# A conv, attention and gated-FFN kernel: t1 centred by its weights, its mean carried in a 129th column, and three steps moved in the written order

## The chip, the cores and the metric

The kernel runs on one core of a Trainium2 chip. Five engines work side by side: TensorE (PE: matmuls; PEld: its weight loads), VectorE (DVE), ScalarE (ACT), GpSimd (POOL) and SyncE (SP, which issues all DMAs here). The metric is the device time of one execution in microseconds (us), lower is better.

## The reference, cut to what matters

```python
x = conv(x)                    # (I - circulant)^-1 over the 128 channels: a 128x128 matrix
t = to_tokens(x)               # 16 batches of 1024 tokens, 128 channels each
t = t + attention(_ln_t(t))    # causal linear attention, 8 heads, then W_out       -> "t1"
t = t + ffn(_ln_t(t))          # per batch: mean gate, merged W1 and W2, LN, gain, bias
x = from_tokens(t)

def _ln_t(v, eps=1e-05):
    m = mean(v, axis=-1); s = var(v, axis=-1)      # over the 128 channels of a token
    return (v - m) / sqrt(s + eps)
```

t1 is used twice: its normalised form z = (t1 - mean) * rstd feeds the gate and the FFN, and t1 itself is added to the FFN's result at the end.

## The kernel before

**Setup** (lines 199 to 364) computes the conv matrix from its filter, folds it into the weights that x meets (`wbig`, split into float16 high and low parts `wh` and `wl`: 128 columns of conv, then 384 of q, k and v), turns W_out into `woT`, and prepares constants. VectorE writes these one after another; a barrier ends it.

**Phase 1** (lines 367 to 1038) goes over 16 batches of 8 tiles of 128 tokens, 128 tiles in all. Each engine runs a written list of stages once per slot; a stage's number is its skew, the slots by which it lags tile t. So a slot is one tile's time, and in slot s a stage of skew k works on tile s - k. The engines meet by semaphores only. The stages that matter here:

- ACT: `v_hi`, `normalise` (z from t1, line 796: an Identity with a scale and a bias that are read per partition), `split_x` (every second slot, even), `tv_hi` (a piece of the FFN's weight share to float16, also even slots), `relu_qk`, `gate_relu` (odd slots), `read_t1` (t1 from PSUM, line 744), `exp_qk`, `state_hi`, two `scores_hi`, `copy_out`.
- DVE: `stats2`, `mean_var2` and `eps2` of t1, `shift2` (line 883: minus mean times rstd, one value a partition), `tv_lo` (line 846), two `scores_lo`, `make_qk`, `v_lo` and others.
- POOL: `split_x` (even slots), `rsqrt2`, `qk_hi` (line 1001), `z_hi` (line 1019), `qk_lo`, `z_lo`, `rsqrt1`.
- PE: `gate` (odd slots), `project`, `state`, `scores`, `turn_out`, `conv`, `values`, `out_project`. `conv` shares a PSUM bank with `out_project`, so it waits until `read_t1` of the slot has read the bank.
- SP: `turn` (q and k to the transposed layout by DMA), `turn_z`, `store` of t1 to DRAM, `load_x`, `load_tv`.

**Phase 2** (lines 1041 to 1438) goes over 32 half batches of 512 tokens, called q, again in slots. PE makes the hidden layer (`up_0` to `up_3`), then `down_0` to `down_3`; each `down` takes the high and low parts of the hidden layer, and the low parts (`h_lo`, line 1369) come from DVE. DVE's order in a slot is

```python
FFN_VECTOR_ORDER = [("copy_b1", 0), ("stats", 2), ("hidden_lo_0", 1), ("hidden_lo_2", 1), ("add_up", 3),
                    ("mean_var", 2), ("add_eps", 2), ("hidden_hi_1", 0), ("copy_w2", 0), ("shift", 2),
                    ("hidden_hi_3", 0), ("hidden_lo_1", 0), ("hidden_lo_3", 0)]
FFN_GPSIMD_ORDER = [("rsqrt", 2), ("gain", 2)]
```

`rsqrt` (line 1433) follows `add_eps`, `shift` (line 1397) follows `rsqrt`, ACT's `normalise` follows `shift`, `gain` (line 1426, POOL, times the LN gain) follows `normalise`, and `add_up` (line 1404, DVE) adds t1, which SP has loaded back from DRAM into `t1b` two half batches ahead.

Of the kernel before, what the change touches and what calls it, by code (L numbers as in the profile page):

```python
# [7 lines left out]
F32 = mybir.dt.float32  # L8
F16 = mybir.dt.float16
# [26 lines left out]
TVW = FO * C // B  # L36
PKW = 2 * (NH * 4 * DH + DH)
# [25 lines left out]
FFN_GPSIMD_ORDER = [("rsqrt", 2), ("gain", 2)]  # L63
# [52 lines left out]
def build(nc, d):  # L116

    top = ExitStack()
    with top:
# [14 lines left out]
        wh = sb(top, "w_in_hi", [P, 4 * C], F16)  # L134
        wl = sb(top, "w_in_lo", [P, 4 * C], F16)
        woT = sb(top, "w_outT", [P, C])
# [62 lines left out]
        with ExitStack() as su:  # L199
# [6 lines left out]
            yt = sb(early, "t1", [P, TILES, C])  # L206
# [9 lines left out]
            wbig = sb(su, "w_in", [P, 4 * C])  # L216
# [4 lines left out]
            with nc.Block() as block:  # L221
# [31 lines left out]
                def _(dve):  # L253
# [51 lines left out]
                    nc.vector.tensor_scalar(wbig[:, C:3 * C], pa[:, 4, 0:2 * C], WSI, None, ALU.mult)  # L305
                    link(nc.vector.tensor_scalar(wbig[:, 3 * C:4 * C], pa[:, 4, 2 * C:3 * C], WSI * VS, None, ALU.mult))
# [60 lines left out]
        with early, ExitStack() as pa_:  # L367
# [28 lines left out]
             t1_ready, bn2, mv2, ve2, rstd2, shift_ready, z_ready, zhi_ready, zlo_ready, gt_done, gate_ready) = [  # L396
# [4 lines left out]
                    "t1_ready bn2 mv2 ve2 rstd2 shift_ready z_ready zhi_ready zlo_ready gt_done gate_ready").split()]  # L401
# [38 lines left out]
            with nc.Block() as block:  # L440
                @block.sync
                def _(sp):
# [77 lines left out]
                def _(pe):  # L520
# [194 lines left out]
                def _(act):  # L715
# [111 lines left out]
                def _(dve):  # L827
# [104 lines left out]
                    def merged_w1(slot):  # L932
# [33 lines left out]
                        "make_qk": make_qk, "shift2": shift2, "state_lo": state_lo,  # L966
# [74 lines left out]
        with ExitStack() as pb:  # L1041
# [11 lines left out]
            t1b = sb(pb, "t1_back", [P, 2, HALF, C])  # L1053
# [62 lines left out]
            with nc.Block() as block:  # L1116
# [181 lines left out]
                def _(dve):  # L1298
# [121 lines left out]
                def _(pool):  # L1420
# [8 lines left out]

                    def rsqrt(g, pair, h):  # L1430
# [7 lines left out]
                    run(pool, FFN_GPSIMD_ORDER, {"rsqrt": rsqrt, "gain": gain})  # L1438
# [30 lines left out]
```

## Time and profile before

| | |
|---|---|
| three runs | 732.48, 734.12, 737.25 us; median 734.12 |
| the profiled execution | 735.35 us, its span 733.4 us |
| granted TensorE clock, mean | 0.983 |
| busy share: PE, DVE, ACT, POOL | 93%, 88%, 86%, 68% |

Lines are those of the kernel before. An instruction's span reaches past the start of the next one on its engine, since instructions overlap at their ends; so the time that one takes from its engine is read from start to start, and sums of spans overstate how full an engine is.

### The profile page before, as it was taken

The numbers are of one execution on the slowest core, as the hardware profiler recorded it, in microseconds if no ns is written. First come the engines' busy times: TensorE is split into PE (matmuls) and PEld (weight loads), VectorE is DVE, ScalarE is ACT, GpSimd is POOL, SyncE is SP. The second block draws the span as 40 slices with busy tenths as digits, with TensorE's granted clock in tenths as the row PEclk, the third lists the DMA queues.
The fourth block names the chain that finished last, engine by engine and source line by source line (L and its number), as shares of the span: only waits on it lengthen the run. The fifth ranks groups of instructions, "written<-read, shape, count | busy, mean of one in ns | idle before, by whom it ended". The sixth has DMA issues, their size and how long they took to land. (4 is left out here: it accounts for less than half of the span.)

```text
span 733.4 us, 39983 instructions
## 1 busy us (share of the span) xinstructions
PE 683.1 (93%) x13026; PEld 531.0 (72%) x13026; DVE 647.6 (88%) x2535; ACT 634.2 (86%) x1780; POOL 498.8 (68%) x911
## 2 busy tenths in 40 slices
PE   3898999999999999999999998889999998999993
PEld 2576777777777777777777776767777797777772
DVE  5689999999999999999999999667998977998983
ACT  3689999999999999999999998457888876888883
POOL 3669999999999999999999997301333312333333
PEclk9999999999999999999999999799999999999998
DMA  4547876666666666666666665210222211222222
GB/s 138 109 111 130 154 139 151 143 147 147 148 138 156 143 144 149 147 152 144 143 149 151 136 142 119 38 37 17 77 83 72 86 44 45 87 72 72 86 86 72
DMA packets 200294, 82.58 MB, mean 113 GB/s; under 512 B 174028, under 2 KB 187503, under 8 KB 200184
## 3 DMA queue, kind: packets, MB, share of 16 engines
q1 hardware_dynamic: 200248, 81.98, 47.7%
q8 instruction: 28, 0.46, 0.3%
q14 instruction: 18, 0.15, 0.1%
HBM read 22.69 MB, written 17.30 MB: 55 GB/s over the span
## 5 line engine op out<-in xcount | busy, mean ns | idle before, releaser
L900 DVE SCALAR_TENSOR_TENSOR scores_lo<-p_a,scores_hi 128x512 f16<-128x512 f32 x256 | 170.6, 677 | 1.2 <-ACT scores_hi L781 1.2
L781 ACT ACTIVATE scores_hi<-p_a 128x512 f16<-128x512 f32 x256 | 162.7, 646 | 4.9 <-PE p_a L617 4.8
L1433 POOL TENSOR_TENSOR ffn_rstd_shift<-ffn_rstd_shift,consts 128x4 f32<-128x4 f32 x32 | 36.8, 1150 | 110.9 <-DVE ffn_rstd_shift L1391 110.9
L1260 ACT ACTIVATE h_f<-psb,merged_b_of_batch 128x512 f32<-128x512 f32 x128 | 87.3, 712 | 11.7 <-PE psb L1196 10.1
L1215 PE MATMUL psb<-merged_W_of_batch,h_hi 128*128 128x128 f16 x512 | 94.5, 220 | 2.3 <-DVE h_lo L1369 1.6
L1369 DVE TENSOR_TENSOR h_lo<-h_f,h_hi 128x512 f16<-128x512 f32 x128 | 95.5, 785 | 1.3 <-ACT h_hi L1271 1.2
L1216 PE MATMUL psb<-merged_W_of_batch,h_hi 128*128 128x128 f16 x512 | 94.2, 220 | 0.0
L1217 PE MATMUL psb<-merged_W_of_batch,h_lo 128*128 128x128 f16 x512 | 94.2, 220 | 0.0
L634 PE MATMUL p_o<-v_parts,scores_hi 128*128 128x17 f16 x1024 | 90.4, 171 | 2.4 <-issue 0.6
L1001 POOL CAST qk_parts<-qk_f 128x512 f16<-128x512 f32 x128 | 78.3, 612 | 17.9 <-issue 15.7
L634 PEld LDWEIGHTS p_o<-v_parts,scores_hi 128*128 128x128 f16 x1024 | 81.6, 96 | 11.8 <-issue 9.2
L638 PE MATMUL p_o<-v_parts,scores_lo 128*128 128x17 f16 x1024 | 89.9, 170 | 0.0
L636 PE MATMUL p_o<-v_parts,scores_hi 128*128 128x16 f16 x1024 | 89.7, 170 | 0.0
L1007 POOL TENSOR_TENSOR qk_parts<-qk_f,qk_parts 128x256 f16<-128x256 f32 x128 | 86.0, 672 | 0.6
L636 PEld LDWEIGHTS p_o<-v_parts,scores_hi 128*128 128x128 f16 x1024 | 80.4, 96 | 0.7 <-issue 0.7
L980 POOL TENSOR_TENSOR stats<-stats,consts 128x1 f32<-128x1 f32 x128 | 70.4, 550 | 15.4 <-DVE stats L853 15.0
L1426 POOL TENSOR_TENSOR normed<-normed,ln_gain_rows 128x512 f32<-128x512 f32 x32 | 40.6, 1269 | 59.0 <-ACT normed L1280 59.0
L638 PEld LDWEIGHTS p_o<-v_parts,scores_lo 128*128 128x128 f16 x1024 | 80.1, 96 | 0.0
L1280 ACT ACTIVATE normed<-psb,ffn_rstd_shift 128x128 f32<-128x128 f32 x128 | 48.2, 457 | 34.0 <-DVE ffn_rstd_shift L1397 34.0
L986 POOL TENSOR_TENSOR stats<-stats,consts 128x1 f32<-128x1 f32 x128 | 70.4, 550 | 4.3 <-DVE stats L859 4.3
L796 ACT ACTIVATE z<-t,stats 128x128 f32<-128x128 f32 x128 | 71.6, 560 | 0.0
L760 ACT ACTIVATE exp_qk<-p_in,stats 128x256 f32<-128x256 f32 x128 | 66.5, 520 | 5.8 <-POOL stats L980 5.0
(214 smaller groups left out, 2775.3 us busy)
## 6 DMA issues: line engine op xcount, KB each, us to landing
x_f<-in_x SPq DMA_DIRECT2D x32, 256.0 KB, 3.0
t_rows<-t SPq DMA_DIRECT2D x64, 128.0 KB, 2.0
t_back<-t_rows SPq DMA_DIRECT2D x32, 256.0 KB, 2.6
out<-out_tile SPq DMA_DIRECT2D x32, 256.0 KB, 2.0
tv_share<-in_L_ffn_tv_W SPq DMA_DIRECT2D x32, 128.0 KB, 2.2
qkT_parts<-qk_parts SPq DMA_TRANSPOSE x128, 3.1
zT_hi_lo<-z_parts SPq DMA_TRANSPOSE x64, 2.4
merged_W<-in_L_ffn_W SPq DMA_DIRECT2D x2, 256.0 KB, 4.3
```

The lines of the kernel that those rows point to most:

```text
L634: mm(num[:, h, :], hi, vp[:, t, h, 0:VW], start=(h == 0), stop=False, skip_group_check=True)
L636: mm(num[:, h, 0:DH], hi, vp[:, t, h, VW:VW + DH], start=False, stop=False, skip_group_check=True)
L638: last = mm(num[:, h, :], lo, vp[:, t, h, 0:VW], start=False, stop=True, skip_group_check=True)
L781: nc.scalar.activation(ah[:, t % 2, cols], p_a[:, cols], ACT.Relu).then_inc(ahi_ready[eo], 1)
L900: nc.vector.scalar_tensor_tensor(al[:, t % 2, cols], p_a[:, cols], 0.0, ah[:, t % 2, cols], ALU.max, ALU.subtract).then_inc(alo_ready[eo], 1)
L1001: nc.gpsimd.tensor_copy(parts_of(t % 4, 0, NH * 4 * DH + DH, 2 * DH), src.unsqueeze(2).broadcast_to([P, 2 * NH, 2, DH])).then_inc(qkhi_rea ...
L1007: nc.gpsimd.tensor_tensor(parts_of(t % 4, 2 * DH, NH * 4 * DH - 2 * DH, DH), qk[:, t % 4, :].rearrange("p (w h i) -> p w h i", w=2, i=DH), ...
L1215: mm(o, hi, w2b[:, bb, 0, c, :], start=False, stop=False)
L1216: mm(o, hi, w2b[:, bb, 1, c, :], start=False, stop=False)
L1217: last = mm(o, lo, w2b[:, bb, 0, c, :], start=False, stop=(c == FC - 1))
L1260: nc.scalar.activation(hf_[:, c, :], ps[:, c, :], ACT.Relu, bias=b1s[:, h // 2, c:c + 1], scale=1.0 / WS).then_inc(h_ready[c], 1)
L1369: nc.vector.tensor_tensor(hl[:, h % 2, c, :], hf_[:, c, :], hh[:, h % 2, c, :], ALU.subtract)\
```

## The change

The conv weights lose their mean over the output channels, W_out likewise, so that t1 comes out of PE without its channel mean. The mean itself is made as a 129th column (`C1` = 129) of the same four matmuls. `read_t1` copies 129 columns, the store to DRAM and the load back carry 1032 bytes for two tiles' rows where they carried 1024, `normalise` needs no bias, and `shift2` is gone. In phase 2 a new POOL step `add_mean` adds the 129th column to t1's 128 in place, before `add_up`. The lists of ACT, DVE and SP are written anew: `tv_hi` lags by one slot (odd slots, with `gate_relu`), `tv_lo` by two, `mean_var2` stands before `v_lo`, `turn` lags by three and stands first on SP.

```diff
-SCALAR_ORDER = [("v_hi", 2), ("normalise", 10), ("split_x", 0), ("tv_hi", 0), ("relu_qk", 2), ("gate_relu", 14),
+SCALAR_ORDER = [("v_hi", 2), ("normalise", 10), ("tv_hi", 1), ("split_x", 0), ("relu_qk", 2), ("gate_relu", 14),
                 ("read_t1", 7), ("exp_qk", 1), ("state_hi", 3), ("scores_hi_0", 4), ("copy_out", 6),
                 ("scores_hi_1", 4)]
-VECTOR_ORDER = [("invert", 6), ("stats2", 8), ("divide", 6), ("make_qk", 2), ("v_lo", 2), ("mean_var2", 8),
-                ("state_lo", 3), ("stats1", 0), ("tv_lo", 0), ("eps2", 8), ("shift2", 9), ("mean_var1", 0),
-                ("scores_lo_0", 4), ("eps1", 0), ("scores_lo_1", 4)]
+VECTOR_ORDER = [("invert", 6), ("stats2", 8), ("divide", 6), ("make_qk", 2), ("mean_var2", 8), ("v_lo", 2),
+                ("state_lo", 3), ("stats1", 0), ("tv_lo", 2), ("eps2", 8), ("mean_var1", 0), ("scores_lo_0", 4),
+                ("eps1", 0), ("scores_lo_1", 4)]
-SYNC_ORDER = [("turn_z", 12), ("store", 7), ("turn", 2), ("load_x", 3), ("load_tv", 1)]
+SYNC_ORDER = [("turn", 3), ("store", 7), ("turn_z", 12), ("load_x", 2), ("load_tv", 1)]
...
-FFN_GPSIMD_ORDER = [("rsqrt", 2), ("gain", 2)]
+FFN_GPSIMD_ORDER = [("add_mean", 2), ("rsqrt", 2), ("gain", 2)]
...
-                    nc.vector.tensor_scalar(wbig[:, 0:C], pa[:, 1, 0:128], WSI, None, ALU.mult)
+                    nc.vector.tensor_scalar(wbig[:, 0:C], pa[:, 1, 128:256], WSI, None, ALU.mult)
+                    link(nc.vector.tensor_reduce(wom[:, 2:3], pa[:, 1, 0:128], AX.X, ALU.add))
+                    nc.vector.tensor_scalar(wbig[:, C:Q0], wom[:, 2:3].broadcast_to([P, Q0 - C]), WSI / C, None, ALU.mult)
                     link(nc.vector.tensor_copy(gfh[:, :], wsqT[:, 4, :]))
                     dve.wait_ge(s_wtc, 1)
-                    nc.vector.tensor_scalar(woT[:, :], wsqT[:, 3, :], WSI, None, ALU.mult)
+                    link(nc.vector.tensor_reduce(wom[:, 0:1], wsqT[:, 3, :], AX.X, ALU.add))
+                    link(nc.vector.tensor_scalar(wom[:, 1:2], wom[:, 0:1], 1.0 / C, None, ALU.mult))
+                    nc.vector.tensor_scalar(woT[:, 0:C], wsqT[:, 3, :], wom[:, 1:2], WSI, ALU.subtract, ALU.mult)
+                    nc.vector.tensor_scalar(woT[:, C:C1], wom[:, 1:2], WSI, None, ALU.mult)
...
-                        o, cols = p_m1[:, 0:P], slice(j * P, (j + 1) * P)
-                        mm(o, xh[:, hf, cols], wh[:, 0:C], start=True, stop=False)
+                        o, cols = p_m1[:, 0:C1], slice(j * P, (j + 1) * P)
+                        mm(o, xh[:, hf, cols], wh[:, 0:C1], start=True, stop=False)
...
-                        nc.scalar.activation(yt[:, t, :], p_m1[:, 0:P], ACT.Copy, scale=1.0 / WSI).then_inc(t1_ready, 1)
+                        nc.scalar.activation(yt[:, t, :], p_m1[:, 0:C1], ACT.Copy, scale=1.0 / WSI).then_inc(t1_ready, 1)
...
-                        act.wait_ge(shift_ready, n + 1)
+                        act.wait_ge(rstd2, n + 1)
                         at_least(act, zlo_ready, n - 1)
-                        nc.scalar.activation(z_[:, t % 2, :], yt[:, t, :], ACT.Identity, bias=st2[:, t % 4, 10:11],
-                                             scale=st2[:, t % 4, 8:9]).then_inc(z_ready, 1)
+                        nc.scalar.activation(z_[:, t % 2, :], yt[:, t, 0:C], ACT.Copy, scale=st2[:, t % 4, 8:9])\
+                            .then_inc(z_ready, 1)
...
-                    def shift2(b, t):
-                        n = TILES * b + t
-                        dve.wait_ge(rstd2, n + 1)
-                        nc.vector.tensor_scalar(st2[:, t % 4, 10:11], st2[:, t % 4, 6:7], -1.0, st2[:, t % 4, 8:9],
-                                                ALU.mult, ALU.mult).then_inc(shift_ready, 1)
...
                         dve.wait_ge(gain_ready, q + 1)
-                        dve.wait_ge(t1_loaded[hf], 16 * (2 * pair + h // 2 + 1))
-                        nc.vector.tensor_tensor(rn[:, hf, :, :], rn[:, hf, :, :], t1b[:, hf, :, :], ALU.add)\
+                        dve.wait_ge(raised, q + 1)
+                        nc.vector.tensor_tensor(rn[:, hf, :, :], rn[:, hf, :, :], t1b[:, hf, :, 0:C], ALU.add)\
                             .then_inc(v_ready, 1)
...
+                    def add_mean(g, pair, h):
+                        q, hf = HB * pair + h, h % 2
+                        pool.wait_ge(t1_loaded[hf], 16 * (2 * pair + h // 2 + 1))
+                        nc.gpsimd.tensor_tensor(t1b[:, hf, :, 0:C], t1b[:, hf, :, 0:C],
+                                                t1b[:, hf, :, C:C1].broadcast_to([P, HALF, C]), ALU.add)\
+                            .then_inc(raised, 1)
...
-                    run(pool, FFN_GPSIMD_ORDER, {"rsqrt": rsqrt, "gain": gain})
+                    run(pool, FFN_GPSIMD_ORDER, {"rsqrt": rsqrt, "gain": gain, "add_mean": add_mean})
```

## Rows read from the trace of the kernel before

**Rows 1.** Windows: PE, PEld, DVE, ACT, POOL busy (instructions); clock; DMA share; GB/s.

```profile
200.00:250.00 50.00, 48.80 (x1162) 38.17 (x1162) 48.70 (x215) 49.76 (x163) 48.34 (x99) 1.00 0.65 149
...
540.00:600.00 60.00, 59.78 (x742) 47.25 (x740) 51.61 (x159) 50.13 (x99) 20.74 (x17) 1.00 0.23 75
```

**Rows 2.** Timeline of ACT, phase 1 (start, length, instruction).

```profile
305.82 0.51 ACT L796 ACTIVATE z<-t,stats 128x128 f32<-128x128 f32 x1
306.20 0.43 ACT L725 ACTIVATE x_hi<-x_f 128x256 f16<-128x256 f32 x1
306.51 0.32 ACT L734 ACTIVATE tv_hi<-tv_share 128x128 f32 x1
306.71 0.46 ACT L767 ACTIVATE p_in<-p_in,stats 128x256 f32<-128x256 f32 x1
...
328.93 0.46 ACT L751 ACTIVATE v_parts<-p_in,stats 128x128 f16<-128x128 f32 x1
355.79 0.46 ACT L751 ACTIVATE v_parts<-p_in,stats 128x128 f16<-128x128 f32 x1
```

**Rows 3.** Waits, 200 to 400 us: total, times, longest.

```profile
POOL qk_parts L1001 <- issue: 7.0, 30, 0.3
...
PEld p_m L557 <- ACT t L744: 3.1, 15, 0.2
```

**Rows 4.** Timeline of POOL, phase 2, one slot (in brackets: idle before, releaser).

```profile
579.65 1.27 POOL L1426 TENSOR_TENSOR normed<-normed,ln_gain_rows 128x512 f32<-128x512 f32 x1 [1.81 <-ACT normed L1280]
583.24 1.14 POOL L1433 TENSOR_TENSOR ffn_rstd_shift<-ffn_rstd_shift,consts 128x4 f32<-128x4 f32 x1 [2.33 <-DVE ffn_rstd_shift L1391]
586.20 1.27 POOL L1426 TENSOR_TENSOR normed<-normed,ln_gain_rows 128x512 f32<-128x512 f32 x1 [1.82 <-ACT normed L1280]
```

**Rows 5.** Timeline of DVE, phase 2, the same slot.

```profile
578.29 1.29 DVE L1369 TENSOR_TENSOR h_lo<-h_f,h_hi 128x512 f16<-128x512 f32 x2
...
580.37 1.71 DVE L1369 TENSOR_TENSOR h_lo<-h_f,h_hi 128x512 f16<-128x512 f32 x2
581.99 0.68 DVE L1404 TENSOR_TENSOR normed<-normed,t_back 128x512 f32<-128x512 f32 x1
582.59 0.37 DVE L1385 BATCH_NORM_AGGREGATE ffn_mean_var<-ffn_stats 128x2 f32<-128x6 f32 x4
583.00 0.17 DVE L1391 TENSOR_SCALAR ffn_rstd_shift<-ffn_mean_var 128x4 f32<-128x4 f32 x1
...
583.57 0.28 DVE L1353 COPY merged_W_of_batch<-merged_W_hi 128x512 f16 x1
```

**Rows 6.** Groups by line, 200 to 400 us: busy, mean ns, idle.

```profile
L796 ACT ACTIVATE z<-t,stats 128x128 f32<-128x128 f32 x60 | 34.3, 572 | 0.0
...
L751 ACT ACTIVATE v_parts<-p_in,stats 128x128 f16<-128x128 f32 x60 | 27.1, 452 | 0.0
...
L744 ACT ACTIVATE t<-p_m 128x128 f32<-128x128 f32 x60 | 19.3, 322 | 0.0
...
L883 DVE TENSOR_SCALAR stats<-stats 128x1 f32<-128x1 f32 x60 | 12.2, 204 | 0.0
```

**Rows 7.** DMA issues of the page (KB each, us to landing).

```profile
t_back<-t_rows SPq DMA_DIRECT2D x32, 256.0 KB, 2.6
...
qkT_parts<-qk_parts SPq DMA_TRANSPOSE x128, 3.1
```

**Rows 8.** Timeline of DVE, setup.

```profile
9.71 0.28 DVE L289 TENSOR_SCALAR cas_scaled<-consts,filter_steps 128x128 f32<-128x128 f32 x1
...
12.04 0.60 DVE L299 TENSOR_SCALAR w_outT<-square_weights_T 128x128 f32<-128x128 f32 x1
```

**Rows 9.** Timelines of POOL and DVE, phase 1: z_hi alone, and beside tv_lo.

```profile
318.31 0.30 POOL L1019 CAST z_parts<-z 128x128 f16<-128x128 f32 x1
...
321.63 0.36 DVE L846 SCALAR_TENSOR_TENSOR tv_lo<-tv_share,tv_hi 128x128 f32 x1
...
321.78 0.36 POOL L1019 CAST z_parts<-z 128x128 f16<-128x128 f32 x1
```

More of the change, by code:

```diff
@@ L36 @@
 TVW = FO * C // B
+C1 = C + 1
+Q0 = C + 16
 PKW = 2 * (NH * 4 * DH + DH)
@@ L133, in build @@
         delta2h = sb(top, "delta2_f16", [P, GB, FI], F16)
-        wh = sb(top, "w_in_hi", [P, 4 * C], F16)
-        wl = sb(top, "w_in_lo", [P, 4 * C], F16)
-        woT = sb(top, "w_outT", [P, C])
+        wh = sb(top, "w_in_hi", [P, Q0 + 3 * C], F16)
+        wl = sb(top, "w_in_lo", [P, Q0 + 3 * C], F16)
+        woT = sb(top, "w_outT", [P, C1])
         gfh = sb(top, "gate1_hi", [P, C], F16)
@@ L205, in build @@
             vp = sb(early, "v_parts", [P, 8, NH, 2 * DH + 1], F16)
-            yt = sb(early, "t1", [P, TILES, C])
+            yt = sb(early, "centred_t1_and_mean", [P, TILES, C1])
             g2n = sb(early, "gate2_rows", [E, C])
@@ L215, in build @@
             casd = sb(su, "cas_scaled", [P, 2, C])
-            wbig = sb(su, "w_in", [P, 4 * C])
+            wbig = sb(su, "w_in", [P, Q0 + 3 * C])
+            wom = sb(su, "w_out_mean", [P, 3])
             cw = sb(su, "centred_inverse", [P, C])
@@ L304, in _ @@
                     dve.wait_ge(s_pch, 3)
-                    nc.vector.tensor_scalar(wbig[:, C:3 * C], pa[:, 4, 0:2 * C], WSI, None, ALU.mult)
-                    link(nc.vector.tensor_scalar(wbig[:, 3 * C:4 * C], pa[:, 4, 2 * C:3 * C], WSI * VS, None, ALU.mult))
+                    nc.vector.tensor_scalar(wbig[:, Q0:Q0 + 2 * C], pa[:, 4, 0:2 * C], WSI, None, ALU.mult)
+                    link(nc.vector.tensor_scalar(wbig[:, Q0 + 2 * C:Q0 + 3 * C], pa[:, 4, 2 * C:3 * C], WSI * VS, None, ALU.mult))
                     link(nc.vector.tensor_copy(wh[:, :], wbig[:, :]))
@@ L395, in build @@
              av_done, den2, o_ready, ot_done, oT_ready, wo_done,
-             t1_ready, bn2, mv2, ve2, rstd2, shift_ready, z_ready, zhi_ready, zlo_ready, gt_done, gate_ready) = [
+             t1_ready, bn2, mv2, ve2, rstd2, z_ready, zhi_ready, zlo_ready, gt_done, gate_ready) = [
                 sem(s) for s in (
@@ L569, in project @@
                         cols = slice(j * P, (j + 1) * P)
-                        mm(p_in[:, t % 2, 0:3 * C], xh[:, hf, cols], wh[:, C:4 * C], start=True, stop=False)
-                        mm(p_in[:, t % 2, 0:3 * C], xh[:, hf, cols], wl[:, C:4 * C], start=False, stop=False)
-                        mm(p_in[:, t % 2, 0:3 * C], xl[:, hf, cols], wh[:, C:4 * C], start=False, stop=True).then_inc(in_done, 1)
+                        mm(p_in[:, t % 2, 0:3 * C], xh[:, hf, cols], wh[:, Q0:Q0 + 3 * C], start=True, stop=False)
+                        mm(p_in[:, t % 2, 0:3 * C], xh[:, hf, cols], wl[:, Q0:Q0 + 3 * C], start=False, stop=False)
+                        mm(p_in[:, t % 2, 0:3 * C], xl[:, hf, cols], wh[:, Q0:Q0 + 3 * C], start=False, stop=True).then_inc(in_done, 1)
                     def state(b, t):
@@ L657, in out_project @@
                         bank_read("out_project", n, t)
-                        o, cols = p_m1[:, 0:P], slice(j * P, (j + 1) * P)
-                        mm(o, xh[:, hf, cols], wh[:, 0:C], start=True, stop=False)
-                        mm(o, xh[:, hf, cols], wl[:, 0:C], start=False, stop=False)
-                        mm(o, xl[:, hf, cols], wh[:, 0:C], start=False, stop=False)
+                        o, cols = p_m1[:, 0:C1], slice(j * P, (j + 1) * P)
+                        mm(o, xh[:, hf, cols], wh[:, 0:C1], start=True, stop=False)
+                        mm(o, xh[:, hf, cols], wl[:, 0:C1], start=False, stop=False)
+                        mm(o, xl[:, hf, cols], wh[:, 0:C1], start=False, stop=False)
                         pe.wait_ge(oT_ready, n + 1)
@@ L920, in stats2 @@
                         dve.wait_ge(t1_ready, n + 1)
-                        nc.vector.bn_stats(st2[:, t % 4, 0:6], yt[:, t, :]).then_inc(bn2, 1)
+                        nc.vector.bn_stats(st2[:, t % 4, 0:6], yt[:, t, 0:C]).then_inc(bn2, 1)
                     def mean_var2(b, t):
@@ L965, in _ @@
                     run(dve, VECTOR_ORDER, {"tv_lo": tv_lo, "stats1": stats1, "mean_var1": mean_var1, "v_lo": v_lo,
-                        "make_qk": make_qk, "shift2": shift2, "state_lo": state_lo,
+                        "make_qk": make_qk, "state_lo": state_lo,
                         "scores_lo_0": scores_lo(0), "scores_lo_1": scores_lo(1),
@@ L1052, in build @@
             hl = sb(pb, "h_lo", [P, 2, FC, 512], F16)
-            t1b = sb(pb, "t1_back", [P, 2, HALF, C])
+            t1b = sb(pb, "t1_back", [P, 2, HALF, C1])
             rn = sb(pb, "normed", [P, 2, HALF, C])
@@ L1061, in build @@
             (b1_ready, gs_ready, g_done, g9r, b12_done, b_chain, gb_ready,
-             w2_copied, f2_done, fbn, fmv, fve, frs, fsh, n_ready, gain_ready, v_ready,
+             w2_copied, f2_done, fbn, fmv, fve, frs, fsh, n_ready, raised, gain_ready, v_ready,
              t_done, ob_ready) = [sem(s) for s in (
                 "b1_ready gs_ready g_done g9_ready b12_done b_chain gb_ready "
-                "w2_copied f2_done fbn fmv fve frs fsh n_ready gain_ready v_ready "
+                "w2_copied f2_done fbn fmv fve frs fsh n_ready raised gain_ready v_ready "
                 "t_done ob_ready").split()]
@@ L1462 @@
         aps[name[3:]] = nc.dram_tensor(name, a.shape, mybir.dt.from_np(a.dtype), kind="ExternalInput").ap()
-    aps["t1"] = nc.dram_tensor("t1_rows", (NHALF * P, HALF * C), F32, kind="Internal").ap()
+    aps["t1"] = nc.dram_tensor("t1_rows", (NHALF * P, HALF * C1), F32, kind="Internal").ap()
     aps["base_parts"] = nc.dram_tensor("base_parts", (2, 2, P, BW), F16, kind="Internal").ap()
```

4 lines of the change are left out of this document (2 added, 2 removed).

## Prediction

> **What bounds the kernel now.** I read the windows first, for a picture by stage. Phase 1 fills the time to about 445 us and shows four engines near full: of 50 us, ACT 49.76, PE 48.80, DVE 48.70, POOL 48.34; phase 2 shows PE 59.78 of 60 and POOL only 20.74 [rows 1]. Neither tells the bound, because spans overlap at their ends. So I read timelines from start to start next. In phase 1 a batch of 8 tiles takes 355.79 - 328.93 = 26.86 us, that is 6.7 us for a pair of slots (even and odd), and ACT's `normalise` takes 306.20 - 305.82 = 0.38 us of it per slot, `tv_hi` 0.20 us in the even slot [rows 2]. The list of waits then shows who is late: in even slots PE's `conv` waits for `read_t1` (15 times in 30 pairs), which on ACT stands behind `normalise`, `split_x`, `tv_hi` and `relu_qk`. So ACT's even slot sets the pair. POOL is nearly full as well: its only steady idle time is 7.0 us in 200, before `qk_hi`, once a pair [rows 3].
>
> Phase 2 is bound by a loop through DVE and POOL, though PE looks full. A slot is 586.20 - 579.65 = 6.55 us, from one `gain` to the next [rows 4]. DVE goes through it in order: two `h_lo` (1.29 us), stats, two more `h_lo`, `add_up`, `mean_var`, `add_eps` at 583.00 [rows 5]; then POOL's `rsqrt` at 583.24, `shift`, ACT's `normalise`, and `gain` [rows 4]. What to see is the second pair of `h_lo`: 1.71 us where the same two took 1.29 [rows 5]. It was issued at 580.37, while `gain` ran from 579.65 to 580.92. The first of the pair lost 0.42 us; it took its normal course only from about 580.79, 0.13 us ahead of `gain`'s end. So a VectorE instruction with two SBUF inputs stands still while such a GpSimd one runs. That lost time is already part of the loop, and the loop has no idle time on DVE except the wait for `rsqrt`.
>
> **Phase 1.** `normalise` loses its bias. The nearest rows for what is left: `v_parts` (one per-partition operand) 452 ns against `t` (none) 322 ns, so one operand costs 130 ns at most; z, with two, has 572 ns [rows 6]. I take 0.09 us off per tile, half of what z's 0.38 us a start has above `tv_hi`'s 0.20 us, which has no such operand and also reads SBUF [rows 2]; the bounds are 0 and 0.13. `tv_hi` leaves the even slot for the odd one: 0.20 us off the slot that PE waits for, 0.20 us on the other. So the even path to `read_t1` becomes 0.29 us shorter, which is more than the wait that it causes. `shift2` (204 ns long [rows 6], some 0.12 us a start) goes from DVE, and with it a step between `rsqrt2` and `normalise`. The 129th column adds one column of 128 to four matmuls and to `read_t1`: under 1% of 322 ns, nothing. Next late is POOL: it can give no more than its idle time, 7.0 us of 200 [rows 3], which over some 400 us of steady batches is 14 us. I take 12 us off. Bounds: 14 us off, and 7 us on, if the odd slot, now with `gate_relu` and `tv_hi`, becomes the long one (0.20 - 0.09 = 0.11 us for each of 60 pairs).
>
> The SP list looks rewritten, but the sequence hardly moves: between one `turn` and the next stand the same `store` or `turn_z`; only the two loads change places, each one turn earlier or later, and what they wait for (POOL's `split_x`, DVE's `tv_lo`) stands ahead of the `qk_lo` that the next `turn` waits for. `turn` lands 3.1 us after issue [rows 7], and its reader `scores` stands two slots behind `qk_lo`, so some tenths of a microsecond more would cost nothing. Moving `tv_lo` and `mean_var2` keeps each in its slot's slack. The longer rows of t1 (1032 bytes for 1024) go through stores that are read a whole batch later, and loads that land in 2.6 us [rows 7]; a load is issued when `add_up` ends (582.67 [rows 5]) and wanted when the next `gain` ends (587.47 [rows 4]), some 2 us after it has landed. All this I cost at nothing; its cover is POOL's pace.
>
> **Setup.** DVE's chain there is continuous to its end. Added: two reductions of 128x128 at 0.28 us [rows 8] plus links, three tiny scalings at about 0.1; `woT` gets cheaper, since at 0.60 us for a 0.28 us shape [rows 8] it had stood still beside POOL. Sum +0.8 us (0.3 to 1.5).
>
> **Phase 2, add_mean.** On POOL it is a 128x512 add like `gain`, 1.27 us, and stands right behind it, where POOL is idle for 2.33 us before `rsqrt` [rows 4]. By POOL's own row it costs nothing. But in that gap DVE runs `h_lo_0` (let go at 580.79), `h_lo_2` and `add_up`, all with two SBUF inputs, back to back until 582.6 [rows 5]. `add_mean` can't run beside them: one of the sides stands still. Which one, no row shows for this pair; the nearest is phase 1, where `tv_lo`, issued at 321.63 ahead of `z_hi` at 321.78, went first, and `z_hi` took 0.36 us for 0.30 [rows 9]. The earlier issued goes first. `add_mean` is issued at about 580.9, behind `h_lo_0` but ahead of `h_lo_2` (581.39). So I take it that `h_lo_2` stands still for it: gain's 1.27 less the 0.13 at its end, less up to 0.14 for a start already made, 1.0 to 1.14, say 1.07 us a slot. `h_lo_2` is in the loop, and `add_up`, `mean_var`, `rsqrt` and PE's `down_0` queue behind it. Of 32 half batches some 29 meet it: the first and the ends of the two groups don't. 29 x 1.07 = 31 us on. Bounds: nothing, and 29 x 1.27 = 37 us.
>
> The Trainium skill, SBUF — State Buffer, section "Who interferes with whom", speaks against the change: VectorE with two SBUF inputs and a GpSimd instruction that reads SBUF share a port under an exclusive lock, the second to issue blocks until the first has finished, and issue order decides. The trace agrees in the stall of 0.42 us [rows 5]. By the rule `add_mean` goes ahead of `h_lo_2`, as in the sum; it doesn't say whether a waiting GpSimd instruction gets in between two VectorE instructions that follow each other closely, on which the first rival rests.
>
> **The rivals.**
> - *VectorE keeps the port* through `h_lo_2` and `add_up`. Then `add_mean` runs from about 582.5 to 583.75, and `rsqrt`, behind it on POOL, starts 0.5 us late. 29 x 0.5 = 14.5 us on instead of 31: 737.5 us, no change. For it: two `h_lo` take 1.29 us together [rows 5], with no gap between them. Against: [rows 9], and POOL has waited since 580.9.
> - *The port is not held*, the rival on the other side: `add_mean` passes beside VectorE as `rsqrt` does, beside which a copy keeps its 0.28 us [rows 4, 5]. It then fits into the 2.33 us at no cost, and only phase 1 and the setup count: 723 us. It decides if `add_mean` takes under 0.4 us a slot from the loop (12 us over 29 slots). Against: `gain`, same shape and inputs, did hold `h_lo_0`.
> - *The gain of phase 1 is not there*: the odd slot becomes the long one, 0 to 7 us on, and phase 2 costs its 31 us: 766 to 773 us.
> - *The change doesn't do what it says*: `normalise` costs the same without its bias. Then only the 0.20 us of `tv_hi` helps; 3 to 4 us of the 12 are lost: 757 us, inside the forecast's own range.
>
> **How the numbers follow.** The profiled execution, 735.35 us (span 733.4 and 1.95 around it), stands 1.2 above the median of the runs. 735.35 + 0.8 - 12 + 31 = 755.2; less 1.2 is 754 us. Its own range is 748 to 761. With 14.5 for 31: 737.5; with 0: 723. Chances: forecast 0.46 (the fourth rival in it), VectorE keeps the port 0.25, port not held 0.21, no gain in phase 1 0.08. About 1% is what a measurement here tells from no change, 726.8 to 741.5. Slower: 0.46 + 0.08 + 0.02 of the first rival's upper end = 0.56; same 0.23; faster 0.21. The range from 722 to 763 leaves out half of the third case and most of the last.
>
> **What would show it.** Right: in phase 2 the gap from one `gain` to the next grows from 6.55 to 7.6 us, `h_lo` next to `add_mean` shows about 1.7 us, PE waits for `h_lo`; in phase 1 a batch takes 26.1 us, z some 480 ns, and POOL's idle time before `qk_hi` is gone. If VectorE keeps the port, `add_mean` shows a long span and `rsqrt` starts late by 0.5. A batch still at 26.8 us would mean that the odd slot took over. A load of t1 that lands later than `gain`'s end would put a wait before `add_mean`.

## The result, and the profile after

The changed kernel takes 752.05 us (median of 6 runs, 748.12 to 754.61) against 734.63 us of the kernel before (6 runs beside it): the ratio is 1.0229, 95% interval 1.0190 to 1.0268. It is slower by 2.3%, and the forecast was 754.

Where the time went is read from two steady stretches, since one execution's ends of phases scatter (POOL's first instruction of phase 2 starts at 471.35 to 473.96 us in six kernels with the same phase 1) while a slot in its steady part repeats to 0.02 us (one or two slots in four are 0.1 to 0.17 us longer, and such slots stand in the kernel before too). In phase 1 the batch of 8 tiles went from 26.82 us (mean of the later batches; 26.86 in the one of [rows 2]) to 26.43. In phase 2 the slot went from 6.55 us [rows 4] to 7.40. Over 15 and 29 of them that is 15 x 0.39 = 5.9 us off and 29 x 0.85 = 24.7 us on. The setup put some 0.7 us on (the first `v_parts` of phase 1 starts at 20.2 to 21.1 us in ten kernels with the new arithmetic, at 19.6 to 20.5 in four with the old). Sum: 19.5 on, where the interval says 14.0 to 19.7 and the spans of the two profiled executions differ by 18.8.

The slot of phase 2, first POOL's timeline (start, length, instruction, in brackets the idle time before and its releaser):

```profile
552.45 1.27 POOL L1428 TENSOR_TENSOR normed<-normed,ln_gain_rows 128x512 f32<-128x512 f32 x1 [1.82 <-ACT normed L1282]
553.67 1.49 POOL L1435 TENSOR_TENSOR t_back<-t_back 128x512 f32<-128x512 f32 x1
556.88 1.14 POOL L1442 TENSOR_TENSOR ffn_rstd_shift<-ffn_rstd_shift,consts 128x4 f32<-128x4 f32 x1 [1.72 <-DVE ffn_rstd_shift L1393]
559.84 1.27 POOL L1428 TENSOR_TENSOR normed<-normed,ln_gain_rows 128x512 f32<-128x512 f32 x1 [1.82 <-ACT normed L1282]
```

and DVE's in the same slot:

```profile
553.17 2.54 DVE L1371 TENSOR_TENSOR h_lo<-h_f,h_hi 128x512 f16<-128x512 f32 x2
555.63 0.68 DVE L1406 TENSOR_TENSOR normed<-normed,t_back 128x512 f32<-128x512 f32 x1
556.24 0.36 DVE L1387 BATCH_NORM_AGGREGATE ffn_mean_var<-ffn_stats 128x2 f32<-128x6 f32 x4
556.63 0.17 DVE L1393 TENSOR_SCALAR ffn_rstd_shift<-ffn_mean_var 128x4 f32<-128x4 f32 x1
...
558.06 0.16 DVE L1399 SCALAR_TENSOR_TENSOR ffn_rstd_shift<-ffn_mean_var,ffn_rstd_shift 128x4 f32<-128x4 f32 x1 [0.36 <-POOL ffn_rstd_shift L1442]
```

POOL's `add_mean` (line 1435) is hidden on POOL: there is still 1.72 us of idle time before `rsqrt`. What grew is the second pair of `h_lo`, 2.54 us where [rows 5] has 1.71. What follows it on DVE up to `shift` keeps its length and is late by as much. The chain that ended last (start, length, what) is now strung on that instruction, about once a slot:

```profile
546.79 1.52 DVE h_lo L1371
554.19 1.52 DVE h_lo L1371
```

The second `h_lo` of the pair takes 1.52 us here, 0.68 in the kernel before, and the starts lie 7.40 us apart: that is the new slot. Next comes the list of waits from 475 to 740 us (total, times, longest), first of the kernel before, then of the changed one, where PE's `down` matmuls wait for `h_lo` in nearly every slot:

```profile
PE psb L1215 <- DVE h_lo L1369: 1.6, 1, 1.6
```

```profile
PE psb L1217 <- DVE h_lo L1371: 25.7, 29, 1.5
```

And an `add_mean` with nothing beside it, the first of the phase, behind its load:

```profile
475.93 1.04 POOL L1435 TENSOR_TENSOR t_back<-t_back 128x512 f32<-128x512 f32 x1 [1.67 <-DMA t_back<-t_rows]
```

It takes 1.04 us alone, not `gain`'s 1.27 [rows 4]; so of the 1.49 that it has in a steady slot 0.45 are waiting, behind the first `h_lo` of the pair. In phase 1 the groups of 300 to 400 us (busy, mean ns, idle) show the cheaper `normalise`:

```profile
L804 ACT ACTIVATE z<-centred_t_and_mean,stats 128x128 f32<-128x128 f32 x30 | 13.3, 445 | 0.0
```

`normalise` takes 445 ns for 572 [rows 6], and from start to start 0.29 us for 0.385: 0.09 us off each, as forecast. The batch lost only 0.39 us, though, where 8 x 0.09 for `normalise` alone would be 0.72, and 0.29 for each of 4 even slots would be 1.16.

### The profile page after: what moved, and what is told of

Same layout as the page of the kernel before. It is cut to its first block and busy times, and to the rows that moved or that the text cites. A ratio compares the mean times of both kernels' runs of the same rounds, so it can differ in the third digit from the quotient of the medians.

```text
span 752.2 us, 39879 instructions
## 1 busy us (share of the span) xinstructions
PE 680.6 (90%) x13026; PEld 530.6 (71%) x13026; DVE 666.4 (89%) x2412; ACT 625.6 (83%) x1780; POOL 541.1 (72%) x943
## 5 line engine op out<-in xcount | busy, mean ns | idle before, releaser
L789 ACT ACTIVATE scores_hi<-p_a 128x512 f16<-128x512 f32 x256 | 157.6, 618 | 7.1 <-PE p_a L625 6.0
L1371 DVE TENSOR_TENSOR h_lo<-h_f,h_hi 128x512 f16<-128x512 f32 x128 | 120.4, 980 | 0.7 <-ACT h_hi L1273 0.6
L1217 PE MATMUL psb<-merged_W_of_batch,h_hi 128*128 128x128 f16 x512 | 95.4, 221 | 25.7 <-DVE h_lo L1371 25.7
L982 POOL TENSOR_TENSOR stats<-stats,consts 128x1 f32<-128x1 f32 x128 | 69.6, 543 | 18.9 <-DVE stats L861 16.7
L1217 PEld LDWEIGHTS psb<-merged_W_of_batch,h_hi 128*128 128x128 f16 x512 | 50.5, 99 | 31.4 <-DVE h_lo L1371 30.9
L988 POOL TENSOR_TENSOR stats<-stats,consts 128x1 f32<-128x1 f32 x128 | 68.9, 538 | 5.0 <-DVE stats L867 5.0
L768 ACT ACTIVATE exp_qk<-p_in,stats 128x256 f32<-128x256 f32 x128 | 63.0, 492 | 4.7 <-POOL stats L982 4.0
```

The costliest lines, as they stand in the source:

```text
L789: nc.scalar.activation(ah[:, t % 2, cols], p_a[:, cols], ACT.Relu).then_inc(ahi_ready[eo], 1)
L1217: mm(o, hi, w2b[:, bb, 0, c, :], start=False, stop=False)
L1371: nc.vector.tensor_tensor(hl[:, h % 2, c, :], hf_[:, c, :], hh[:, h % 2, c, :], ALU.subtract)\
```

## The experiments

### Phase 2: what add_mean costs, and why

**Without it.** The mean is not added back.

```diff
-FFN_GPSIMD_ORDER = [("add_mean", 2), ("rsqrt", 2), ("gain", 2)]
+FFN_GPSIMD_ORDER = [("rsqrt", 2), ("gain", 2)]
...
-                        dve.wait_ge(raised, q + 1)
+                        dve.wait_ge(t1_loaded[hf], 16 * (2 * pair + h // 2 + 1))
```

> The changed kernel without add_mean: the mean is not added back in phase 2, so that part of the computation is left out, and add_up waits for the load of t1 itself. Port theory (add_mean stands VectorE's second pair of h_lo still, 0.91 us a slot over 28 slots = 25.5 us): phase 2 falls back to about 253.5 us and the time to about 752.0 - 25.5 = 726.5 us; the second pair of h_lo goes back from 2.62 to 1.71 us. Rival, the longer rows of t1 (1032 bytes, a later landing, a strided operand) or the new order of the wait are what phase 2 pays for: then 740 to 752 us.

Measured: 728.37 us, ratio 0.9937 (0.9911 to 0.9963); slot 6.55 us, second pair of `h_lo` back at its old length:

```profile
557.05 1.70 DVE L1371 TENSOR_TENSOR h_lo<-h_f,h_hi 128x512 f16<-128x512 f32 x2
```

So `add_mean` is the whole of phase 2's cost. The longer rows of t1, their later landing and the moved wait cost nothing that shows. The ratio also gives what phase 1 brings, net of the setup: 4.6 us, 2.7 to 6.5 by its interval.

**As long, but without reading.** A one-column add takes the wait, and a memset has the length (0.95 us). The mean is not added back.

```diff
+            idle = sb(pb, "written_only", [P, 1025])
...
-                        nc.gpsimd.tensor_tensor(t1b[:, hf, :, 0:C], t1b[:, hf, :, 0:C],
-                                                t1b[:, hf, :, C:C1].broadcast_to([P, HALF, C]), ALU.add)\
-                            .then_inc(raised, 1)
+                        nc.gpsimd.tensor_tensor(idle[:, 1024:1025], t1b[:, hf, 0, 0:1], t1b[:, hf, 0, C:C1], ALU.add)
+                        nc.gpsimd.memset(idle[:, 0:1024], 0.0).then_inc(raised, 1)
```

> The changed kernel with add_mean replaced by a GpSimd memset of 128x1024 (about 1 us, it reads no SBUF) behind a one-column add that takes the wait; the mean is not added back, that part is left out. Port theory: POOL is busy for as long, but VectorE isn't stood still: h_lo back at 1.71 us, about 726 to 729 us. Rival, POOL's own time and order cost it (rsqrt late behind a 1 us operation, add_up late behind its signal): about 750 us, with h_lo short and rsqrt's wait longer.

Measured: 727.80 us, ratio 0.9931 (0.9905 to 0.9958), slot 6.55 us. POOL's and DVE's timelines:

```profile
561.72 0.64 POOL L1436 TENSOR_TENSOR written_only<-t_back 128x1 f32<-128x1 f32 x1
562.29 0.95 POOL L1437 MEMSET written_only<- 128x1024 f32 x1
```

```profile
561.20 1.70 DVE L1372 TENSOR_TENSOR h_lo<-h_f,h_hi 128x512 f16<-128x512 f32 x2
562.83 0.68 DVE L1407 TENSOR_TENSOR normed<-normed,t_back 128x512 f32<-128x512 f32 x1
```

POOL is busy as long, in the same place, with the same signal behind it, and nothing is slower. Beside the memset DVE's two-input instructions keep their 1.70 and 0.68 us. So it is neither POOL's time nor its order nor `add_up`'s wait, but what the add reads. The Trainium skill, SBUF — State Buffer, section "Who interferes with whom", has it so: a VectorE instruction with two SBUF inputs contends with a GpSimd instruction that reads SBUF, not with one that only writes. This pair of runs agrees, with 1.70 us for 2.54.

**Behind rsqrt instead of ahead of it.** The computation is whole.

```diff
-FFN_GPSIMD_ORDER = [("add_mean", 2), ("rsqrt", 2), ("gain", 2)]
+FFN_GPSIMD_ORDER = [("rsqrt", 2), ("add_mean", 2), ("gain", 2)]
```

> The changed kernel with GpSimd's list turned so that add_mean is issued behind rsqrt and ahead of gain, beside the later hi copies and the first pair of h_lo and not in the gap before rsqrt. Theory that the place in the list is the fault (add_mean in the rsqrt loop): about 727 us, because POOL is idle there for 1.7 us while ACT normalises. Port theory: the hold only moves from the second pair of h_lo to the work of VectorE that now lies beside it; shift and the first h_lo pair are in the same loop, so 740 to 752 us, and the second pair of h_lo is back at 1.71 us.

Measured: 752.64 us, ratio 1.0283 (1.0233 to 1.0332), slot 7.39 us. POOL's and DVE's timelines:

```profile
562.94 1.03 POOL L1435 TENSOR_TENSOR t_back<-t_back 128x512 f32<-128x512 f32 x1
```

```profile
558.86 1.78 DVE L1371 TENSOR_TENSOR h_lo<-h_f,h_hi 128x512 f16<-128x512 f32 x2
...
563.00 1.00 DVE L1399 SCALAR_TENSOR_TENSOR ffn_rstd_shift<-ffn_mean_var,ffn_rstd_shift 128x4 f32<-128x4 f32 x1 [0.91 <-POOL ffn_rstd_shift L1442]
563.92 0.41 DVE L1363 CAST h_hi<-h_f 128x512 f16<-128x512 f32 x1
```

The place in the list is not the fault: the same 0.84 us has moved. `shift`, an instruction of four columns that took 0.16 us, started 0.06 us behind `add_mean` and took 1.00, until `add_mean` had ended. The second pair of `h_lo`, here without `add_mean` beside it, is back at 1.78. `shift` is in the loop too, so the slot is the same to 0.01 us.

**The mean added on VectorE**, by four `scalar_tensor_tensor` in place of `add_up`'s one instruction; the computation is whole.

```diff
-FFN_GPSIMD_ORDER = [("add_mean", 2), ("rsqrt", 2), ("gain", 2)]
+FFN_GPSIMD_ORDER = [("rsqrt", 2), ("gain", 2)]
...
-                        dve.wait_ge(raised, q + 1)
-                        nc.vector.tensor_tensor(rn[:, hf, :, :], rn[:, hf, :, :], t1b[:, hf, :, 0:C], ALU.add)\
-                            .then_inc(v_ready, 1)
+                        dve.wait_ge(t1_loaded[hf], 16 * (2 * pair + h // 2 + 1))
+                        for j in range(HALF):
+                            last = nc.vector.scalar_tensor_tensor(rn[:, hf, j, :], t1b[:, hf, j, 0:C], t1b[:, hf, j, C:C1],
+                                                                  rn[:, hf, j, :], ALU.add, ALU.add)
+                        last.then_inc(v_ready, 1)
```

> The changed kernel with the mean added on VectorE instead: add_up becomes four scalar_tensor_tensor of 128x128 (t1 + mean column + normalised), GpSimd has no add_mean. Full computation. Port theory: no hold, but four instructions for one in the loop, some 0.2 to 0.3 us a slot more in add_up: 726.5 + 29 x 0.25 = about 733 us. Theory that the mean's work itself costs wherever it is put: about 750 us.

Measured: 740.52 us, ratio 1.0128 (1.0074 to 1.0183); 7 us above what was expected. The four take

```profile
558.53 1.13 DVE L1407 SCALAR_TENSOR_TENSOR normed<-t_back,normed 128x128 f32<-128x128 f32 x4
```

1.13 us where `add_up` took 0.68 [rows 5], and the slot is 7.00 us: all of the 0.45 us is in the loop (29 x 0.45 = 13 us). The mechanism held; the price had been put at half.

**The mean added on ScalarE**, where ACT waits for `shift`; the computation is whole.

```diff
-FFN_GPSIMD_ORDER = [("add_mean", 2), ("rsqrt", 2), ("gain", 2)]
+FFN_GPSIMD_ORDER = [("rsqrt", 2), ("gain", 2)]
...
+                    def add_mean(g, pair, h):
+                        q, hf = HB * pair + h, h % 2
+                        act.wait_ge(t1_loaded[hf], 16 * (2 * pair + h // 2 + 1))
+                        for j in range(HALF):
+                            last = nc.scalar.activation(t1b[:, hf, j, 0:C], t1b[:, hf, j, 0:C], ACT.Identity,
+                                                        bias=t1b[:, hf, j, C:C1], scale=1.0)
+                        last.then_inc(raised, 1)
...
-FFN_SCALAR_ORDER = [("hidden_3", 0), ("hidden_1", 0), ("hidden_hi_0", 0), ("hidden_0", 0), ("normalise", 2),
+FFN_SCALAR_ORDER = [("hidden_3", 0), ("hidden_1", 0), ("hidden_hi_0", 0), ("hidden_0", 0), ("add_mean", 2), ("normalise", 2),
```

> The changed kernel with the mean added on ScalarE: four activations of 128x128 (t1 plus its mean column as bias) ahead of normalise in ACT's list of phase 2, where ACT waits 1.06 us a slot for shift; GpSimd has no add_mean. Full computation. Port theory: ACT takes no part in the port that VectorE and GpSimd share, so the second pair of h_lo is back at 1.7 us; four activations take about 1.0 us from start to start (0.25 us each, as v_parts), which the wait hides: 727 to 730 us. Rival (ACT's wait isn't spare, since hidden_2 and hidden_hi_2 behind it come later): up to 1 us a slot, 740 to 755 us.

Measured: 730.26 us, ratio 0.9972 (0.9954 to 0.9990): the one full version that is faster than the kernel before by its interval, though by 0.3% only. ACT's timeline:

```profile
560.47 0.78 ACT L1262 ACTIVATE h_f<-psb,merged_b_of_batch 128x512 f32<-128x512 f32 x1
561.04 1.36 ACT L1281 ACTIVATE t_back<-t_back 128x128 f32<-128x128 f32 x4
562.40 1.51 ACT L1290 ACTIVATE normed<-psb,ffn_rstd_shift 128x128 f32<-128x128 f32 x4
```

The four take 1.36 us, not 1.0, and fill ACT's wait to its end: `normalise` follows with no gap. So the slot is 6.60 us, 0.05 over the one before (29 x 0.05 = 1.5 us).

### Phase 1: where the other half of the gain went

**tv_hi alone moved**, in the kernel before.

```diff
-SCALAR_ORDER = [("v_hi", 2), ("normalise", 10), ("split_x", 0), ("tv_hi", 0), ("relu_qk", 2), ("gate_relu", 14),
+SCALAR_ORDER = [("v_hi", 2), ("normalise", 10), ("tv_hi", 1), ("split_x", 0), ("relu_qk", 2), ("gate_relu", 14),
...
-                ("state_lo", 3), ("stats1", 0), ("tv_lo", 0), ...
+                ("state_lo", 3), ("stats1", 0), ("tv_lo", 2), ...
```

> The kernel before with tv_hi alone moved (one tile later, ahead of x_hi, so that it falls into the odd slot) and tv_lo two tiles later behind it; nothing else of the change. Theory of the prediction (ACT's even slot up to read_t1 sets the pair): 0.20 us for each of some 60 pairs, 12 us off, 723 to 727 us, the start of phase 2 at 468 to 472 us for 479.85. Rival (PE's conv of the even slot waits as much for x_lo, which stands on POOL behind rsqrt1 and z_lo and doesn't move with ACT): 0 to 3 us off, 731 to 735 us, phase 2 from 477 to 480 us.

Measured: 730.77 us, ratio 0.9984 (0.9965 to 1.0003); batch 26.77 us, 0.05 off. The even slots fell from 3.29 us to 3.08 and the odd ones rose from 3.46 to 3.66. To see why, the even slot before (ACT, POOL, PE):

```profile
319.51 0.45 ACT L725 ACTIVATE x_hi<-x_f 128x256 f16<-128x256 f32 x1
319.82 0.34 ACT L734 ACTIVATE tv_hi<-tv_share 128x128 f32 x1
...
320.37 0.32 ACT L744 ACTIVATE t<-p_m 128x128 f32<-128x128 f32 x1
...
320.09 0.68 POOL L1033 TENSOR_TENSOR x_lo<-x_f,x_hi 128x256 f16<-128x256 f32 x1
...
321.04 0.23 PE L557 MATMUL p_m<-w_in_hi,x_hi 128*128 128x128 f16 x1
```

and with `tv_hi` moved:

```profile
317.67 0.46 ACT L725 ACTIVATE x_hi<-x_f 128x256 f16<-128x256 f32 x1
318.33 0.33 ACT L744 ACTIVATE t<-p_m 128x128 f32<-128x128 f32 x1
...
318.24 0.67 POOL L1033 TENSOR_TENSOR x_lo<-x_f,x_hi 128x256 f16<-128x256 f32 x1
...
319.18 0.23 PE L557 MATMUL p_m<-w_in_hi,x_hi 128*128 128x128 f16 x1
```

From the end of `read_t1` (line 744) to `conv` (line 557) it was 321.04 - 320.69 = 0.35 us and is now 319.18 - 318.66 = 0.52; from `x_lo`'s end it is 0.27 in both. It is so in all four even slots of a batch: the distance from `x_lo` is the same to 0.02 us in both kernels (0.24 to 0.27 us in three of them, 0.12 and 0.10 in the fourth), that from `read_t1` is 0.17 to 0.20 longer. `conv` waits for `x_lo`, not for `read_t1`. And `x_lo` starts 0.13 and 0.11 us behind the end of `x_hi`, which stands ahead of where `tv_hi` was.

**The arithmetic alone**, with the lists of the kernel before and the mean added on VectorE (the diff of the change without the four lists, and that of the VectorE version).

> The change's arithmetic (t1 without its mean, normalise without a bias, shift2 gone) with the lists of the kernel before, and the mean added on VectorE in four instructions in phase 2, which cost 12 to 13 us there. Theory of the prediction: 0.09 us off each normalise, in the path of the even slot: 60 x 0.09 = 5 us off phase 1, phase 2 from 475 us, 742 us in all. Rival (ACT isn't what conv waits for last): phase 2 from 478 to 480 us, 745 to 748 us.

Measured: 743.07 us, ratio 1.0150 (1.0126 to 1.0174); batch 26.47 us, 0.35 off: that is 4 x 0.09, one `normalise` for each pair of slots. In the odd slot its 0.09 us runs into a wait for PE's `gate` matmuls, as ACT's timeline shows:

```profile
320.11 0.44 ACT L804 ACTIVATE z<-centred_t_and_mean,stats 128x128 f32<-128x128 f32 x1
320.40 0.48 ACT L775 ACTIVATE p_in<-p_in,stats 128x256 f32<-128x256 f32 x1
321.14 0.47 ACT L815 ACTIVATE gate_hidden<-p_m,gate_b 128x256 f32<-128x256 f32 x1 [0.26 <-PE p_m L683]
...
324.03 0.43 ACT L733 ACTIVATE x_hi<-x_f 128x256 f16<-128x256 f32 x1
```

The kernel before, in the odd slot behind the even one shown above:

```profile
323.30 0.47 ACT L807 ACTIVATE gate_hidden<-p_m,gate_b 128x256 f32<-128x256 f32 x1
...
326.28 0.43 ACT L725 ACTIVATE x_hi<-x_f 128x256 f16<-128x256 f32 x1
```

These two starts cut a pair of slots in two. From `gate_relu` (the row `gate_hidden`) to the next `x_hi` it takes 326.28 - 323.30 = 2.98 us before and 324.03 - 321.14 = 2.89 here; the means of the pairs between 210 and 425 us are 2.97 and 2.88, 2.96 with `tv_hi` alone moved and 2.88 in the whole change. From `x_hi` to the next `gate_relu`, by way of `x_lo`, `conv` and PE's `gate`, the means are 3.74 us before, 3.74 with `tv_hi` moved, 3.73 here and 3.73 in the whole change. One `normalise` stands in the first stretch; the other one and `tv_hi`, in its old place and in its new one, stand in the second, whose mean length stayed within 0.01 us whatever ACT did in it.

**The lists alone**, all four, with the arithmetic of the kernel before (the list part of the change's diff).

> The kernel before with all the changed lists (tv_hi and tv_lo later, mean_var2 ahead of v_lo, SyncE's list) and its own arithmetic: normalise keeps its bias, t1 its mean. Theory of the prediction: tv_hi's 0.20 us leaves the path of the even slot, 8 to 12 us off, phase 2 from 468 to 472 us, 723 to 727 us. Rival (x_lo on POOL): 0 to 3 us off, phase 2 from 477 to 480 us. If the lists alone bring phase 2 to 473 us as the whole change does, the arithmetic was worth nothing and this version, at about 727 us, beats both kernels.

Measured: 729.66 us, ratio 0.9978 (0.9956 to 1.0000); batch 26.76 us, 0.06 off, the same as `tv_hi` alone. So the gain of phase 1 is the arithmetic's; the lists bring a tenth of what was forecast for them.

**tv_hi moved and POOL made lighter**: both `rsqrt` of phase 1 are replaced, so the normalisations scale by zero.

```diff
-                        nc.gpsimd.tensor_tensor(s[:, 8:9], s[:, 9:10], mhalf, ALU.pow).then_inc(rstd1, 1)
+                        nc.gpsimd.tensor_tensor(s[:, 8:9], s[:, 9:10], s[:, 9:10], ALU.subtract).then_inc(rstd1, 1)
...
```

> The kernel before with tv_hi moved to the odd slot (which alone took 0.06 us off a batch of 26.83 us), and with GpSimd made lighter in phase 1: rsqrt1 and rsqrt2 subtract their input from itself instead of raising it to -1/2, so both normalisations of phase 1 scale by zero; that part of the computation is left out. Theory that x_lo on POOL is what conv of the even slot waits for: rsqrt1 ahead of it is 0.35 us shorter, x_lo comes as much earlier, read_t1 is no longer late, and the batch falls by some 0.4 to 0.8 us to 26.0 to 26.4 us. Theory that ACT is simply full over a pair: the batch stays at 26.7 us.

Measured: 732.80 us in one run (734.30 for the kernel before beside it); batch 26.74 us. My theory that POOL's chain makes `x_lo` late fell: `rsqrt1` (line 980) takes 0.19 us for 0.55, and POOL then waits for ACT:

```profile
318.76 0.19 POOL L980 TENSOR_TENSOR stats<-stats 128x1 f32<-128x1 f32 x1
319.25 0.67 POOL L1033 TENSOR_TENSOR x_lo<-x_f,x_hi 128x256 f16<-128x256 f32 x1 [0.30 <-ACT x_hi L725]
```

`conv` starts at 320.19, again 0.27 us behind `x_lo`. What makes `x_lo` late is `x_hi` on ACT: with POOL free, `x_lo` starts 0.08 us behind its end, so `rsqrt1` had held it up by 0.05 and 0.03 us only. That fits all these runs: one `normalise` of each pair stands between the wait for `gate` and `x_hi` and counts, `tv_hi` stands behind `x_hi` in the old place, and ahead of the wait for `gate` in the new one, and counts in neither. The other theory, that ACT is simply full over a pair, gives the same 26.7 us here; but it would have let the arithmetic alone take 8 x 0.09 = 0.72 us off a batch, and that run lost 0.35.

**eps1 earlier**, in the version with the mean on VectorE.

```diff
-("mean_var1", 0), ("scores_lo_0", 4), ("eps1", 0), ("scores_lo_1", 4)]
+("mean_var1", 0), ("eps1", 0), ("scores_lo_0", 4), ("scores_lo_1", 4)]
```

> The variant with the mean added on VectorE (740.5 us, phase 2 from 471.7 us) with eps1 taken out from behind the first scores_lo in VectorE's list. Theory that conv of the even slot waits for eps1, rsqrt1 and x_lo in a chain: rsqrt1 then follows z_lo on POOL at once, up to 0.1 us for each of 60 pairs, 2 to 6 us off: 735 to 738 us, phase 2 from 466 to 470 us. Rival (POOL or ACT is simply full there): no change, 740 us, phase 2 from 471 to 472 us.

Measured: 747.26 us, ratio 1.0238 (1.0202 to 1.0274): slower by some 7 us, against both expectations. The batch is 26.85 us. From 200 to 400 us PE waits longer for `scores_lo`, 5.1 us in 14 times, which were 2.5 in 8 (first the version with the mean on VectorE, then this one):

```profile
PE p_a L616 <- DVE scores_lo L902: 2.5, 8, 0.3
```

```profile
PE p_a L616 <- DVE scores_lo L902: 5.1, 14, 0.4
```

`eps1` needs `mean_var1`, right ahead of it, so what stands behind it on DVE is later: the second `scores_lo` starts 0.90 us behind `mean_var1` (mean from 200 to 400 us), which was 0.75. From `x_hi` to `gate_relu` it is now 3.83 us for 3.73, and 4 x 0.10 us a batch is the whole gain of phase 1. So DVE's order, too, can make that stretch longer.

**POOL or VectorE lighter**, in the whole change. POOL: both `rsqrt` of phase 1 as in the diff above. VectorE: `stats1` and `stats2` read 16 of 128 columns.

> The changed kernel with GpSimd made lighter in phase 1: rsqrt1 and rsqrt2 subtract their input from itself instead of raising it to -1/2 (0.54 us each before), so that both normalisations of phase 1 scale by zero; that part of the computation is left out. If POOL with x_lo on it is what is next late in phase 1 (prediction), the batch of 8 tiles falls from 26.43 us towards what ACT's own work needs, 26.1 us or less; if VectorE's order sets it, it stays at 26.4 us.

> The changed kernel with VectorE made lighter in phase 1: stats1 and stats2 read 16 of their 128 columns (0.30 and 0.24 us before, some 0.1 us less each), so the statistics of both normalisations are those of 16 columns; the rest of them is left out. If VectorE's order sets the pair in phase 1, the batch falls from 26.43 us by up to 8 x 0.2 = 1.6 us, as far as ACT lets it (26.1 us); if POOL sets it, it stays at 26.4 us.

Measured, one run each: 747.96 us and 750.46 us; batch 26.30 and 26.29 us for 26.43. Each gives some 0.14 us of the 0.3 expected at most, and for it POOL had given up 8 x 0.70 us a batch. Both make the stretch from `x_hi` to `gate_relu` shorter, 3.73 us in the whole change, 3.70 with POOL lighter, 3.69 with VectorE lighter: `x_lo` starts 0.51 and 0.53 us behind the start of `x_hi`, where it was 0.55. Neither engine by itself is what is next late.

## Why the prediction was right, and where its terms were off

**Phase 2, right in its mechanism.** The forecast's step was that `add_mean`, issued behind `h_lo_0` and ahead of `h_lo_2`, gets the port first, that `h_lo_2` stands still for it, and that `add_up`, `rsqrt` and `down_0` queue behind. The trace shows each of the three: `add_mean` running ahead of `h_lo_2`, the pair of `h_lo` at 2.54 us, and the chain and PE's 25.7 us of waits strung on it. The memset shows that reading is the condition, the move behind `rsqrt` that the place in the list isn't. The rival in which VectorE keeps the port is excluded by the same rows: `rsqrt` still starts 0.25 us behind `add_eps` (0.24 before [rows 4, 5]), and `add_eps` is what comes later. That the nearest row, `z_hi` beside `tv_lo` [rows 9], pointed the right way is no proof of the rule: `z_hi` took only 0.06 us longer there.

**Its size.** The term was 1.07 us a slot, from `gain`'s 1.27; it measured 0.85. `add_mean` alone takes 1.04 us, though it has `gain`'s shape and form; less what the forecast took off, the 0.13 at its end and up to 0.14 for a start already made, that is 0.77 to 0.91. The term of 31 us became 24.7.

**Phase 1, the step that failed.** "So ACT's even slot sets the pair", because PE's `conv` waits for `read_t1`: that was read from a list that puts a wait for several semaphores down to one [rows 3]. `x_lo` and `read_t1` ended 0.08 us apart, and it is `x_lo` that `conv` waits for. So of ACT's even slot only what stands ahead of `x_hi` is on the path. Of the 0.29 us, `normalise`'s 0.09 counts and `tv_hi`'s 0.20 does not: the even slot fell by 0.21 us and the odd one rose by 0.20, as the rival of the long odd slot had it for `tv_hi`. The term was 12 us off; it measured 15 x 0.39 = 5.9, of which the arithmetic is 0.35 and the lists 0.06 to 0.04 a batch. POOL, named as next late, was not, though the sign that was to tell it came: its 7.0 us of idle time before `qk_hi` [rows 3] are nearly gone in the same 200 us,

```profile
POOL qk_parts L1003 <- issue: 1.1, 7, 0.2
```

but with both its `rsqrt` made some 0.35 us shorter a batch of the change lost 0.13 us.

**Setup** at 0.8 us (some 0.7 measured) held in its sum. `woT` did fall from 0.60 to 0.29 us; but a new scaling of 16 columns took 0.65 us in the same place, beside the same POOL instruction. The edits that were costed at nothing (SP's list, the longer rows, `tv_lo`, `mean_var2`) cost nothing that shows: without `add_mean` the slot of phase 2 is 6.55 us, and with the lists alone phase 1 is not slower.

The two errors, 6 us too much gained and 6 too much lost, cancelled in the sum; that it came within 2 us of the measurement is luck. The range of 722 to 763 us would have held either alone.

What stays open: what sets the rest of the stretch from `x_hi` to `gate_relu`. From `conv` to `gate_relu` it takes 2.28 to 2.30 us in every one of these kernels, and no run took work of PE away there. In one pair of four of the kernel before, ACT itself runs from `x_hi` to `gate_relu` without a wait (3.65 us), so it is not far from setting the time there. That the loop of phase 1 runs through ACT, POOL, PE and DVE by turns is argued from the runs, not shown.

## What to carry to other kernels

An engine's idle time is free only for work that takes nothing from a neighbour: ahead of putting a two-input GpSimd instruction into a gap, look at what VectorE reads in that gap, or give the work to ScalarE. Where a list names one releaser of a wait for two things, measure from the end of each to the start in several slots: the one with the constant distance is the releaser (here 0.27 us for `x_lo` in both kernels, 0.35 and 0.52 for `read_t1` in the same slot). And of an engine's list only what stands between the instruction that it waits for and the one that lets the next engine go is on the path.

## What the runs showed of the hardware beyond that

- A waiting GpSimd instruction gets in between two VectorE instructions that follow each other without a gap: `add_mean`, issued while the first `h_lo` of a pair ran, ran ahead of the second in 29 of the 32 half batches, with a span of 1.48 to 1.49 us in each of them; in the other three, with no `h_lo` beside it, it took 1.04.
- The time lost didn't depend on the size of the held instruction: `shift` with four columns took 1.00 us for 0.16, `h_lo` with 512 columns 1.52 for 0.68.
- Of two GpSimd instructions of 128x512 in float32, the add whose second operand is a column repeated along the row took 1.04 us, the multiply with a whole row repeated for each tile 1.27. Which of the two differences makes it, no run shows.
- In phase 1 an Identity on ACT with a scale and a bias read per partition took 0.385 us of the engine for 128x128, a Copy with the scale alone 0.29.
